# Key and query projections of the single-head layers as three products of rounded parts made on GpSimd

## The chip, the cores and the metric

The kernel runs on one core of one Trainium2 chip, as a single launch. The metric is the device time of that launch in microseconds (us); the figure for a kernel is the median of its runs. Engines are named PE (TensorE, matrix products; PEld is its weight loading), DVE (VectorE), ACT (ScalarE), POOL (GpSimd) and SP (SyncE, which only issues transfers here).

## The reference, cut to what matters

Four attention layers run one after another over 8 images of 128 channels and 1024 positions. The first two have 8 heads of 16 channels, the last two have one head of 128 channels. In a single-head layer, with `P = 128` channels `C` and `N = 1024` positions:

```python
h = _group_norm(x, gamma, beta).reshape(B, Cc, N)
q = jnp.einsum('oc,bcn->bon', wq, h) + bq[None, :, None]
k = jnp.einsum('oc,bcn->bon', wk, h) + bk[None, :, None]
v = jnp.einsum('oc,bcn->bon', wv, h) + bv[None, :, None]
attn = jax.nn.softmax(jnp.einsum('bcn,bcm->bnm', q, k) * scale, axis=-1)
out = jnp.einsum('bcm,bnm->bcn', v, attn)
return x + (jnp.einsum('oc,bcn->bon', wo, out) + bo[None, :, None]).reshape(B, Cc, H, W)
```

## The kernel before, in words

`many_heads` runs layers 0 and 1, `one_head` (line 847 on) layers 2 and 3. The change is in `one_head` alone. It goes through 16 images (2 layers of 8), in a software pipeline: while PE computes attention for one image, it also computes averages, keys, queries and values of the next one. The first image's keys and queries are made at the end of `many_heads`, so 15 images are projected in `one_head`.

The attention of one image is 8 tiles of 128 positions. In the order in which PE's queue is written out (`body` on line 1364), a tile m has: the scores of tile m+2 into `s_ps` (six products, since both operands are kept as a rounded part `HI` and a rest `LO` of type fp32r, and HI*HI, HI*LO and LO*HI are added), eight transposes of tile m's probabilities into `t_ps`, and a quarter of the output product `pv_ps` (six products again). DVE takes the maxima and the rests of the transposed probabilities (`rests`, line 1143). ACT computes exponentials, divides them by their sums and copies the rounded parts (line 1286).

Work for the next image shares one PSUM bank, `misc`, and is placed between these by a table on line 868: `"avg"` in tile 0, `"k0"` at the end of tile 1, `"k1"` at the end of tile 2, `"q0"` at the end of tile 3, `"v0"` in tile 5, `"q1"` at the end of tile 6, `"v1"` in tile 7. Here k0 is the first half (512 positions) of the keys, k1 the second. For the first image, two output products of layer 1 (`o0`, `o1`) are placed in tiles 3 and 4 as well.

How a projection comes about: PE averages the statistics (`average`), DVE computes the variance, POOL makes the scale and the shift (`coefficients`, line 1023), ACT normalises both halves of `x_in` into `h` (line 1229) and raises `h_ready`, PE waits for `h_ready` in front of k0 and computes `project` (line 1313), an fp32 product of 128x128 weights from `wg` with 128x512 of `h`. ACT adds the bias into `full` one tile later (`evacuate`, line 1242) and POOL splits the result into `HI` and `LO` (`split`, lines 1033 and 1034), which the scores of the next image read.

Every engine works through its own queue in order; semaphores join them.

Of the kernel before, what the change touches and what calls it, by code (L numbers as in the profile page):

```python
# [15 lines left out]
ALU = mybir.AluOpType  # L16
ACT = mybir.ActivationFunctionType
AX = mybir.AxisListType
F32 = mybir.dt.float32
BF16 = mybir.dt.bfloat16  # L20
F32R = mybir.dt.float32r

P = 128
T = 1024
B = 8
HALF = 512
# [820 lines left out]
def one_head(nc, ctx0, kept, w, bv, out):  # L847
# [24 lines left out]
    HI, LO = 0, 1  # L872
# [19 lines left out]
    with ctx:  # L892
        def sb(name, shape, dt=F32):
            return ctx.enter_context(nc.sbuf_tensor("o_" + name, shape, dt))
# [4 lines left out]
        def sem(name):  # L899
            return ctx0.enter_context(nc.semaphore("o_" + name))  # L900
# [8 lines left out]
        wg = [sb(f"wg{i}", [P, NW]) for i in range(2)]  # L909
        value_weights = kept["value_weights"]  # L910
        h = sb("h", [P, T])
        y = sb("y", [P, T])
        ident = sb("ident", [P, P])
        bst = sb("bst", [P, 2, 6])
# [43 lines left out]
        coef_ready = sem("coef_ready")  # L958
        scale_ready = sem("scale_ready")
        h_ready = sem("h_ready")  # L960
        x_dma = sem("x_dma")
        w_dma = [sem(f"w_dma{i}") for i in range(2)]
        o_dma = sem("o_dma")
# [54 lines left out]
        @block.gpsimd  # L1018
        def _(pool):
            own = Own(pool, pool_own)  # L1020
            nc.gpsimd.tensor_scalar(ident[:, :], kept["ident"][:, :], 1.0, None, ALU.mult).then_inc(consts, 1)

            def coefficients(n, par):

                pool.wait_ge(coef_ready, n)
                tt = nc.gpsimd.tensor_tensor
                own.done(tt(co[:, 4:5], co[:, 1:2], exponent[:, :], ALU.pow))
                own.done(tt(co[:, 2:3], co[:, 4:5], wg[par][:, W_GAMMA:W_GAMMA + 1], ALU.mult))
                own.done(tt(co[:, 5:6], gs[:, 0:1], co[:, 2:3], ALU.mult))
                tt(co[:, 3:4], wg[par][:, W_BETA:W_BETA + 1], co[:, 5:6], ALU.subtract).then_inc(scale_ready, 1)  # L1030

            def split(source, hi, lo, ready):
                own.done(nc.gpsimd.tensor_copy(hi, source))
                nc.gpsimd.tensor_tensor(lo, source, hi.bitcast(F32), ALU.subtract).then_inc(ready, 1)

            def split_kq(n, operand, name, c):
                pool.wait_ge(kq_full, n)
                cols = slice(c * HALF, (c + 1) * HALF)
                split(full[name][:, cols], operand[:, HI, cols], operand[:, LO, cols], kq_parts)

            def split_v(par, c):
                tiles = slice(c * HT, (c + 1) * HT)
                split(full["v"][:, c * HALF:(c + 1) * HALF].rearrange("p (s c) -> p s c", s=HT),
                      vT[par][:, HI, tiles, :], vT[par][:, LO, tiles, :], v_parts)

            def stage_g(u, par, finish=False):
                coefficients(u + 1, par)
                if finish:
                    pool.wait_ge(rrep_ready, 1)
                    own.done(nc.gpsimd.tensor_tensor(attn[:, :], kept["num"][:, :], kept["rrep"][:, :], ALU.mult))  # L1050
                    pool.sem_inc(attn_ready, 1)
                split_kq(4 * u + 1, k[par], "k", 0)
                split_kq(4 * u + 2, k[par], "k", 1)
                split_kq(4 * u + 3, q[par], "q", 0)
                pool.wait_ge(v_full, 2 * u + 1)
                split_v(par, 0)
                split_kq(4 * u + 4, q[par], "q", 1)
                pool.wait_ge(v_full, 2 * u + 2)
                split_v(par, 1)

            split_v(0, 0)
            split_v(0, 1)
            own.drain()

            def body(first=False, last=False):
                for u in range(2 - last):
                    stage_g(u, 1 - u, finish=first and u == 0)
                if not last:
                    pool.sem_inc(coef_ready, -2)
                    pool.sem_inc(kq_full, -8)  # L1070
                    pool.sem_inc(v_full, -4)
                own.drain()

            body(first=True)
            with pool.Fori(1, PAIRS - 1):
                body()
            body(last=True)

        @block.vector
# [229 lines left out]

        @block.tensor  # L1310
        def _(pe):
            def project(par, c, column):
                nc.tensor.matmul(misc[:, :], wg[par][:, column:column + P], h[:, c * HALF:(c + 1) * HALF],  # L1313
                                 start=True, stop=True).then_inc(misc_for_act, 1)

            def project_values(c):
                for n in range(4):
# [12 lines left out]
            def split_product(to, stationary, moving, start=True, stop=True):  # L1330

                pairs = ((HI, HI), (HI, LO), (LO, HI))
                for n, (a, b) in enumerate(pairs):
                    last = nc.tensor.matmul(to, stationary(a), moving(b), start=start and n == 0,  # L1334
                                            stop=stop and n == len(pairs) - 1)
                return last
# [26 lines left out]

            def body(first=False, last=False):
                places, _, before, taken = shared_bank(first, last)
                for m in range(BODY):
                    u, tile = m // TILES, m % TILES

                    def in_shared_bank(place):

                        name = places[u].get((tile, place))
                        if name is None:
                            return
                        reader, count = before[u, name]
                        pe.wait_ge(misc_act if reader == "act" else misc_dve, count)
                        if name == "avg":
                            pe.wait_ge(stats_ready, u + 1)
                            pe.wait_ge(w_dma[1 - u], 16)
                            combine_weights(nc, misc, wg[1 - u])
                            average()  # L1380
                        elif name == "o0":
                            pe.wait_ge(attn_ready, 1)
                            project_output(0)
                        elif name == "o1":
                            project_output(1)
                        elif name[0] == "v":
                            project_values(int(name[1]))
                        else:
                            if name == "k0":
                                pe.wait_ge(h_ready, u + 1)  # L1390
                            project(1 - u, int(name[1]), W_K if name[0] == "k" else W_Q)

                    pe.wait_ge(p_ready, m + 1)
                    if tile == 2:
                        pe.wait_ge(kq_parts, 4 * u + 1)
                    if tile == TILES - 2 and not (last and u == 1):
                        pe.wait_ge(kq_parts, 4 * u + 4)
                    if not (last and m >= BODY - 2):
                        scores((m + 2) // TILES % 2, m + 2)
                    in_shared_bank(0)  # L1400
                    for bank in range(2):
                        pe.wait_ge(t_free, 2 * m + bank + 1)
                        for n in range(HT):
                            st = bank * HT + n
                            transposed = nc.tensor.transpose(t_ps[bank][:, n, :], probs[m % 2][:, st * P:(st + 1) * P], ident[:, :])  # L1405
                        transposed.then_inc(t_ready, 1)
                    in_shared_bank(1)
                    if m >= HT or not first:
                        if m % HT == 0:
                            pe.wait_ge(pv_free, m // HT + 1)  # L1410
                        if tile == HT:
                            pe.wait_ge(v_parts, 2 * (u + 1))
                        products((m // HT + 3) % 4, m % HT)
                    in_shared_bank(2)
                pe.sem_inc(t_free, -2 * BODY)
                pe.sem_inc(pv_free, -4)
                pe.sem_inc(misc_dve, -taken["dve"])
                pe.sem_inc(misc_act, -taken["act"])
                if not last:
                    pe.sem_inc(p_ready, -BODY)  # L1420
                    pe.sem_inc(kq_parts, -8)
                    pe.sem_inc(v_parts, -4)
                    pe.sem_inc(stats_ready, -2)
                    pe.sem_inc(h_ready, -2)
                    pe.sem_inc(w_dma[0], -16)
                    pe.sem_inc(w_dma[1], -16)

# [102 lines left out]
```

## Time and profile before

| | |
|---|---|
| median of 3 runs | 2296.9 us (2295.36 to 2297.52) |
| span of the profiled execution | 2295.6 us; no other time of that execution is given |
| busy share of the span | PE 96%, PEld 42%, DVE 79%, ACT 75%, POOL 23% |
| `one_head` | about the last 580 us of the span |

The span runs from the first to the last instruction. A busy share is the time in which an engine had an instruction in it, over the whole span; the two halves of the kernel differ, so the rows below are read by stretch. The span lies 1.3 us below the median of the runs.

### The profile page before, as it was taken

What the parts mean: (1) busy time and instruction counts of PE and PEld (TensorE: products, weight loads), DVE (VectorE), ACT (ScalarE), POOL (GpSimd) and SP (SyncE); (2) the same over time, 40 slices, a digit from 0 to 9 for tenths busy, and PEclk for the clock granted to TensorE, in tenths of its full rate; (3) what the DMA queues carried; (4) which work ended last, traced back from release to release, by engine and by line L of the source; (5) the groups of instructions that cost most, each with busy time, mean ns of one, the idle gap of its engine ahead of it and who ended that gap; (6) DMA issues with size and microseconds to landing.
All of it is one profiled execution on the core that took longest, in us unless ns stands there. A gap on an engine that the chain in (4) does not pass through costs nothing. (4 is left out here: it accounts for less than half of the span.)

```text
span 2295.6 us, 34006 instructions
## 1 busy us (share of the span) xinstructions
PE 2201.2 (96%) x11776; PEld 972.2 (42%) x11776; DVE 1815.8 (79%) x3176; ACT 1719.9 (75%) x3107; POOL 520.6 (23%) x689
## 2 busy tenths in 40 slices
PE   3999999999999999999999999999989999999998
PEld 1223232323333232333333232333326888888887
DVE  2878888888888878888888888888837777777776
ACT  1467677777877777776767777776777888888887
POOL 3113030202213030311203020211113333333331
PEclk9999999999999999999999999999999999999999
DMA  6053351606244261616345160615112112121111
GB/s 82 7 70 53 58 78 35 104 22 91 41 69 66 45 90 36 95 27 84 50 61 76 36 103 22 94 37 75 26 31 72 53 48 66 36 65 57 42 53 49
DMA packets 81647, 132.31 MB, mean 58 GB/s; under 512 B 17632, under 2 KB 50528, under 8 KB 81504
## 3 DMA queue, kind: packets, MB, share of 16 engines
q1 hardware_dynamic: 78240, 129.70, 32.5%
q8 instruction: 79, 1.29, 0.3%
q10 hardware_dynamic: 3264, 0.79, 0.2%
q14 instruction: 64, 0.52, 0.1%
HBM read 53.12 MB, written 17.83 MB: 31 GB/s over the span
## 5 line engine op out<-in xcount | busy, mean ns | idle before, releaser
L447 DVE TENSOR_REDUCE h_half_nmax<-h_s_ps 128x1 f32<-128x512 f32 x2048 | 1285.8, 684 | 270.2 <-PE h_s_ps L682 263.0
L598 ACT ACTIVATE h_probs<-h_st_ps 128x512 f32<-128x512 f32 x2048 | 1103.7, 600 | 388.2 <-PE h_st_ps L819 382.2
L682 PE MATMUL h_s_ps<-h_krep,h_qrep 96*128 96x512 bf16 x2048 | 795.7, 389 | 22.4 <-SPq L232 20.8
L819 PE MATMUL h_st_ps<-h_qrep,h_krep 99*128 99x512 bf16 x2048 | 779.9, 382 | 35.1 <-DMA h_qrep<-h_mrow 24.3
L674 PE MATMUL h_pv<-h_probs,h_vT 128*32 128x512 f32 x4096 | 548.1, 607 | 0.9 <-ACT h_probs L598 0.7
L682 PEld LDWEIGHTS h_s_ps<-h_krep,h_qrep 96*128 96x128 bf16 x2048 | 200.0, 98 | 677.3 <-DVE h_half_nmax L447 503.0
L819 PEld LDWEIGHTS h_st_ps<-h_qrep,h_krep 99*128 99x128 bf16 x2048 | 201.7, 99 | 230.6 <-DMA h_qrep<-h_mrow 36.4
L347 POOL TENSOR_SCALAR h_nparts<-h_nmax 128x16 bf16<-128x16 f32 x64 | 16.4, 256 | 956.6 <-DVE h_nmax L455 956.6
L1334 PE MATMUL o_s<-o_k,o_q 128*128 128x512 f32 x768 | 225.7, 430 | 7.4 <-DVE o_q L1155 5.8
L1334 PE MATMUL o_pv<-o_pT,o_vT 128*128 128x512 f32 x768 | 208.1, 406 | 0.8 <-ACTq L1261 0.8
L1149 DVE TENSOR_TENSOR o_pT<-o_t,o_pT 128x512 fp32r<-128x512 f32 x256 | 164.5, 684 | 43.8 <-ACT o_pT L1286 41.4
L1135 DVE TENSOR_REDUCE o_nmax<-o_s 128x1 f32<-128x1024 f32 x128 | 156.4, 1222 | 51.1 <-PE o_s L1334 48.7
L1256 ACT ACTIVATE o_probs<-o_probs,o_rinv 128x1024 f32<-128x1024 f32 x128 | 147.7, 1154 | 38.0 <-DVE o_rinv L1141 22.6
L1334 PEld LDWEIGHTS o_s<-o_k,o_q 128*128 128x128 f32 x768 | 146.6, 191 | 66.5 <-issue 30.2
L674 PEld LDWEIGHTS h_pv<-h_probs,h_vT 128*32 128x32 f32 x4096 | 81.6, 108 | 219.0 <-ACT h_probs L598 158.8
L1250 ACT ACTIVATE o_probs<-o_s,o_bias 128x1024 f32<-128x1024 f32 x128 | 144.3, 1128 | 9.2 <-DVE o_bias L1136 8.7
L1334 PEld LDWEIGHTS o_pv<-o_pT,o_vT 128*128 128x128 f32 x768 | 135.0, 189 | 24.2 <-DVE o_pT L1149 1.2
L1286 ACT CAST o_pT<-o_t 128x512 fp32r<-128x512 f32 x256 | 135.0, 578 | 1.6 <-PE o_t L1405 1.6
L1405 PE MATMUL o_t<-o_ident,o_probs 128*128 128x128 f32 x1024 | 133.2, 273 | 2.3 <-DVE o_pT L1149 2.3
L1405 PEld LDWEIGHTS o_t<-o_ident,o_probs 128*128 128x128 f32 x1024 | 119.2, 141 | 21.0 <-issue 2.5
L648 PE MATMUL h_misc<-h_h,h_wg 128*128 128x512 f32 x136 | 73.7, 623 | 7.9 <-ACT h_h L542 5.4
L328 POOL TENSOR_TENSOR h_co<-h_co,exponent 128x1 f32<-128x1 f32 x17 | 9.7, 568 | 235.9 <-DVE h_co L413 235.9
(116 smaller groups left out, 1380.1 us busy)
## 6 DMA issues: line engine op xcount, KB each, us to landing
h_krep<-h_kp SPq DMA_DIRECT2D x96, 256.0 KB, 8.7
h_qrep<-h_qp SPq DMA_DIRECT2D x192, 128.0 KB, 9.5
x_res<-out_dram SPq DMA_DIRECT2D x24, 512.0 KB, 3.7
num<-av SPq DMA_DIRECT2D x128, 64.0 KB
rrep<-rden_dram SPq DMA_DIRECT2D x16, 512.0 KB
out_dram<-o_y SPq DMA_DIRECT2D x16, 512.0 KB
out_dram<-h_y SPq DMA_DIRECT2D x15, 512.0 KB, 2.6
o_x_in<-out_dram SPq DMA_DIRECT2D x15, 512.0 KB, 3.5
```

The lines of the kernel that those rows point to most:

```text
L447: reduce = nc.vector.tensor_reduce(half_nmax[:, c, unit:unit + 1], s_ps[bank(2 * n + c)][:, :], AX.X, ALU.max, negate=True)
L598: nc.scalar.activation(probs[g % 2][:, j, :], st_ps[bank(n)][:, :], ACT.Exp, scale=1.0 / CH ** 0.5).then_inc(exp_done, 1)
L674: product = nc.tensor.matmul(pv_ps[32 * j:32 * j + 32, :], vT[par][:, k % TILES, quad * QUAD + j, :], probs[k % 2][:, j, :], start=(k % TI ...
L682: nc.tensor.matmul(s_ps[bank(n)][:, :], qrep[par][0:KS, th, head, tile * P:(tile + 1) * P], krep[par][0:KS, head, c * HALF:(c + 1) * HALF] ...
L819: nc.tensor.matmul(st_ps[bank(n)][:, :], krep[par][0:KM, head, st * P:(st + 1) * P], qrep[par][0:KM, th, head, :], start=True, stop=True). ...
L1135: own.done(nc.vector.tensor_reduce(nmax[:, b:b + 1], s_ps[b][:, :, :], AX.XY, ALU.max, negate=True))
L1149: nc.vector.tensor_tensor(pt[:, LO, :, :][to], t_ps[bank][:, :, :], pt[:, HI, :, :][to].bitcast(F32), ALU.subtract).then_inc(t_free, 1)
L1250: nc.scalar.activation(probs[b][:, :], s_ps[b][:, :, :], ACT.Exp, bias=bias[:, b:b + 1], scale=SCALE, accum_out=rsum[:, b:b + 1]).then_inc ...
L1256: nc.scalar.activation(probs[b][:, :], probs[b][:, :], ACT.Copy, scale=rinv[:, b:b + 1]).then_inc(p_ready, 1)
L1286: nc.scalar.copy(pT[m // HT % 2][:, HI, bank * HT:(bank + 1) * HT, m % HT * P:(m % HT + 1) * P], t_ps[bank][:, :, :]).then_inc(hi_ready, 1)
L1334: last = nc.tensor.matmul(to, stationary(a), moving(b), start=start and n == 0, stop=stop and n == len(pairs) - 1)
L1405: transposed = nc.tensor.transpose(t_ps[bank][:, n, :], probs[m % 2][:, st * P:(st + 1) * P], ident[:, :])
```

## The change

Keys and queries are no longer one fp32 product. The weights of keys and queries (128x256) and the normalised `h` (128x1024) are each split into `HI` and `LO` parts of type fp32r, and `project` adds three products of them. POOL makes the parts in the new function `split_projection`: the weights' parts right after the coefficients, then, after a wait for `h_ready`, those of `h` in two halves, each of which raises `h_parts_ready`. PE waits for the first half in front of k0 and for the second in front of k1. The values are still projected from `h` in fp32.

```diff
@@ -909,6 +909,8 @@
         wg = [sb(f"wg{i}", [P, NW]) for i in range(2)]
         value_weights = kept["value_weights"]
         h = sb("h", [P, T])
+        h_parts = sb("h_parts", [P, 2, T], F32R)
+        w_parts = sb("w_parts", [P, 2, 2 * P], F32R)
         y = sb("y", [P, T])
         ident = sb("ident", [P, P])
         bst = sb("bst", [P, 2, 6])
@@ -958,6 +960,7 @@
         coef_ready = sem("coef_ready")
         scale_ready = sem("scale_ready")
         h_ready = sem("h_ready")
+        h_parts_ready = sem("h_parts_ready")
         x_dma = sem("x_dma")
         w_dma = [sem(f"w_dma{i}") for i in range(2)]
         o_dma = sem("o_dma")
@@ -1043,8 +1046,19 @@
                 split(full["v"][:, c * HALF:(c + 1) * HALF].rearrange("p (s c) -> p s c", s=HT),
                       vT[par][:, HI, tiles, :], vT[par][:, LO, tiles, :], v_parts)
 
+            def split_projection(u, par):
+
+                weights = wg[par][:, 0:2 * P]
+                own.done(nc.gpsimd.tensor_copy(w_parts[:, HI, :], weights))
+                own.done(nc.gpsimd.tensor_tensor(w_parts[:, LO, :], weights, w_parts[:, HI, :].bitcast(F32), ALU.subtract))
+                pool.wait_ge(h_ready, u + 1)
+                for c in range(2):
+                    cols = slice(c * HALF, (c + 1) * HALF)
+                    split(h[:, cols], h_parts[:, HI, cols], h_parts[:, LO, cols], h_parts_ready)
+
             def stage_g(u, par, finish=False):
                 coefficients(u + 1, par)
+                split_projection(u, par)
                 if finish:
                     pool.wait_ge(rrep_ready, 1)
                     own.done(nc.gpsimd.tensor_tensor(attn[:, :], kept["num"][:, :], kept["rrep"][:, :], ALU.mult))
@@ -1067,6 +1081,7 @@
                     stage_g(u, 1 - u, finish=first and u == 0)
                 if not last:
                     pool.sem_inc(coef_ready, -2)
+                    pool.sem_inc(h_ready, -2)
                     pool.sem_inc(kq_full, -8)
                     pool.sem_inc(v_full, -4)
                 own.drain()
@@ -1309,9 +1324,10 @@
 
         @block.tensor
         def _(pe):
-            def project(par, c, column):
-                nc.tensor.matmul(misc[:, :], wg[par][:, column:column + P], h[:, c * HALF:(c + 1) * HALF],
-                                 start=True, stop=True).then_inc(misc_for_act, 1)
+            def project(c, column):
+                cols = slice(c * HALF, (c + 1) * HALF)
+                split_product(misc[:, :], lambda part: w_parts[:, part, column:column + P],
+                              lambda part: h_parts[:, part, cols]).then_inc(misc_for_act, 1)
 
             def project_values(c):
                 for n in range(4):
@@ -1386,9 +1402,9 @@
                         elif name[0] == "v":
                             project_values(int(name[1]))
                         else:
-                            if name == "k0":
-                                pe.wait_ge(h_ready, u + 1)
-                            project(1 - u, int(name[1]), W_K if name[0] == "k" else W_Q)
+                            if name in ("k0", "k1"):
+                                pe.wait_ge(h_parts_ready, 2 * u + int(name[1]) + 1)
+                            project(int(name[1]), W_K if name[0] == "k" else W_Q)
 
                     pe.wait_ge(p_ready, m + 1)
                     if tile == 2:
@@ -1421,7 +1437,7 @@
                     pe.sem_inc(kq_parts, -8)
                     pe.sem_inc(v_parts, -4)
                     pe.sem_inc(stats_ready, -2)
-                    pe.sem_inc(h_ready, -2)
+                    pe.sem_inc(h_parts_ready, -4)
                     pe.sem_inc(w_dma[0], -16)
                     pe.sem_inc(w_dma[1], -16)
```

## Rows read from the trace of the kernel before

**Rows 1.** Busy time in a stretch, one image long (engine, instructions; granted clock)

```profile
1873.37:1908.44 35.07, 35.07 (x192) 28.62 (x191) 27.21 (x54) 30.99 (x49) 12.55 (x17) 1.00 0.17 55
```

**Rows 2.** Groups by line, PE, 1760 to 2250 us (busy, mean ns | idle before)

```profile
L1313 PE MATMUL o_misc<-o_h,o_wg 128*128 128x512 f32 x112 | 57.2, 592 | 0.0
```

**Rows 3.** Timeline of PE, a tile without projection (start, length, instruction)

```profile
1890.57 1.04 PE L1405 MATMUL o_t<-o_ident,o_probs 128*128 128x128 f32 x8
1891.37 1.63 PE L1334 MATMUL o_pv<-o_pT,o_vT 128*128 128x512 f32 x6
1892.83 1.55 PE L1334 MATMUL o_s<-o_k,o_q 128*128 128x512 f32 x6
1894.22 1.04 PE L1405 MATMUL o_t<-o_ident,o_probs 128*128 128x128 f32 x8
```

**Rows 4.** Timeline of all engines, from the coefficients to the first keys' parts

```profile
1911.31 0.19 POOL L1030 TENSOR_TENSOR o_co<-o_wg,o_co 128x1 f32<-128x1 f32 x1
1911.54 1.53 ACT L1229 ACTIVATE o_h<-o_x_in,o_co 128x512 f32<-128x512 f32 x2 [0.87 <-POOL o_co L1030]
...
1912.11 1.04 PE L1405 MATMUL o_t<-o_ident,o_probs 128*128 128x128 f32 x8
...
1914.37 1.02 PE L1313 MATMUL o_misc<-o_h,o_wg 128*128 128x512 f32 x2
...
1914.92 1.29 DVE L1149 TENSOR_TENSOR o_pT<-o_t,o_pT 128x512 fp32r<-128x512 f32 x2 [1.19 <-ACT o_pT L1286]
...
1916.37 0.70 ACT L1242 ACTIVATE full_k<-o_misc,o_wg 128x512 f32<-128x512 f32 x1
...
1916.61 1.03 PE L1405 MATMUL o_t<-o_ident,o_probs 128*128 128x128 f32 x8
...
1917.25 0.61 POOL L1033 CAST o_k<-full_k 128x512 fp32r<-128x512 f32 x1 [5.75 <-ACTq L1245]
...
1917.94 1.30 POOL L1034 TENSOR_TENSOR o_k<-full_k,o_k 128x512 fp32r<-128x512 f32 x1
```

**Rows 5.** The same timeline, one image later

```profile
1946.59 1.52 ACT L1229 ACTIVATE o_h<-o_x_in,o_co 128x512 f32<-128x512 f32 x2 [0.75 <-POOL o_co L1030]
...
1949.37 0.59 PE L1313 MATMUL o_misc<-o_h,o_wg 128*128 128x512 f32 x1
```

**Rows 6.** Timeline of PE, the first two products after a wait

```profile
1728.47 0.72 PE L1334 MATMUL o_s<-o_k,o_q 128*128 128x512 f32 x2 [1.65 <-ACT o_probs L1256]
...
1728.79 0.40 PE L1334 MATMUL o_s<-o_k,o_q 128*128 128x512 f32 x1
```

**Rows 7.** Timeline of all engines, first image of the single-head layers

```profile
1735.49 1.52 ACT L1229 ACTIVATE o_h<-o_x_in,o_co 128x512 f32<-128x512 f32 x2 [0.76 <-POOL o_co L1030]
...
1737.17 0.30 PEld L1313 LDWEIGHTS o_misc<-o_h,o_wg 128*128 128x128 f32 x2 [0.93 <-issue]
...
1740.31 0.70 ACT L1242 ACTIVATE full_k<-o_misc,o_wg 128x512 f32<-128x512 f32 x1
1740.39 2.37 POOL L1050 TENSOR_TENSOR attn<-num,rrep 128x1024 f32<-128x1024 f32 x1 [4.94 <-SPq L989]
...
1745.11 0.70 PE L1324 MATMUL o_misc<-attn,wo 128*128 128x512 f32 x1 [0.68 <-ACTq L1244]
```

**Rows 8.** Timeline of all engines, where the single-head layers begin

```profile
1717.89 2.30 POOL L1034 TENSOR_TENSOR o_vT<-full_v,o_vT 128x512 fp32r<-128x512 f32 x1
1718.98 2.29 DVE L1155 TENSOR_TENSOR o_q<-full_q,o_q 128x1024 fp32r<-128x1024 f32 x1
```

**Rows 9.** Timeline of PE in the multi-head layers, waits

```profile
857.28 0.39 PE L819 MATMUL h_st_ps<-h_qrep,h_krep 99*128 99x512 bf16 x1 [1.91 <-DMA h_qrep<-h_mrow]
...
1061.16 0.39 PE L819 MATMUL h_st_ps<-h_qrep,h_krep 99*128 99x512 bf16 x1 [1.81 <-DMA h_qrep<-h_mrow]
```

**Rows 10.** Busy time in stretches of the multi-head layers, granted clock third from last

```profile
160.00:1060.00 900.00, 882.34 (x4824) 280.38 (x4821) 757.25 (x1283) 673.32 (x1290) 179.04 (x239) 1.00 0.41 62
...
1061.00:1066.00 5.00, 4.83 (x18) 1.25 (x19) 2.02 (x4) 2.22 (x4) 0.00 (x0) 0.66 0.37 139
```

## The prediction

> **What bounds the kernel now.** The change is in the single-head layers, so I read those by stretch, not the whole span. First the busy times of a stretch that is one image long: PE is busy for all of its 35.07 us, at full clock (1.00), while DVE has 27, ACT 31 and POOL 12.6 us of work [rows 1]. Then the groups by line on PE: over 490 us the projections had no idle time in front of them, so no wait ends late there [rows 2]. So in a settled image PE's own work is the time: what leaves PE's queue shortens the image, and a wait in PE's queue lengthens it by as much, since there is no slack to absorb it. The third view is the timeline, for two questions: what one projection costs on PE, and how soon after `h` is ready PE reads it.
>
> **The change part by part.**
>
> *The products.* Between the transposes of two tiles without a projection PE takes 1894.22 - 1890.57 = 3.65 us [rows 3]; with k0 in between, 1916.61 - 1912.11 = 4.50 us [rows 4]. An fp32 projection thus costs 0.85 us. It becomes three fp32r products of 128x512, a form that the kernel already uses, each with a weight load of its own: six for the scores take 1894.22 - 1892.83 = 1.39 us, six for the output 1892.83 - 1891.37 = 1.46 us [rows 3], so 0.232 to 0.243 each, and three 0.70 to 0.73. I take the scores (same operands, same two-part pattern): a saving of 0.155 us a projection, with bounds of 0.12 (the output's pace) and 0.17 (the reading of four times to a hundredth). Four projections an image: 0.62 us (0.48 to 0.68).
>
> *The weights' parts.* POOL begins them when the coefficients are done, 1911.31 + 0.19 = 1911.50 [rows 4]. Subtractions of 128x512 take 1.30 us [rows 4] and a two-input operation of 128x1024 2.37 [rows 7], so 256 columns come to about 0.75 us; the cast is under the 0.61 us of 512 columns. With 0.08 us between instructions (0.69 from cast to subtraction, less 0.61 [rows 4]) they end by 1913.1 at the latest. ACT normalises until 1911.54 + 1.53 = 1913.07 and POOL hears of it some 0.1 us later (below). So I cost them at nothing: the normalisation covers them. Were it shorter, all that sticks out would add to the wait that follows.
>
> *The wait.* k0 now follows not ACT but ACT and then POOL. From the end of the normalisation: the signal to POOL; 0.69 us to the start of the subtraction; 1.30 us of subtraction; the signal to PE; and the slower first product after a pause, whose successor follows after 0.32 us [rows 6] where 0.23 is the pace, so 0.09. For the signals the rows give 0.04 us (POOL to ACT, 1911.50 to 1911.54 [rows 4]), 0.16 (ACT to PE, 1737.01 to 1737.17 [rows 7]) and 0.18 (ACT to POOL, 1917.07 to 1917.25 [rows 4]). I take 0.16 for ACT to POOL, where two semaphore steps lie in between as for PE, and 0.09 for POOL to the product, as the instruction itself raises that semaphore. Sum: 0.16 + 0.69 + 1.30 + 0.09 + 0.09 = 2.33 us. So k0 could start at 1913.07 + 2.33 = 1915.40 and started at 1914.37 [rows 4]: 1.03 us late. In the next image it is 1946.59 + 1.52 + 2.33 = 1950.44 against 1949.37 [rows 5]: 1.07. Mean 1.05 us. Lower bound with both signals at 0.04 and no slow restart, 0.78; upper with 0.18 and 0.19, 1.17.
>
> Behind the wait in PE's queue stand k0, the scores of tile 4 and all that follows, so the image gets longer by it. ACT's evacuation of k0 was at 1916.37, after its exponentials [rows 4]; three products from 1915.40 end about 1916.3, so ACT hardly waits. POOL's parts of the second half of `h` follow the first at once and end 1915.22 + 0.03 + 0.69 + 1.30 = 1917.24; k1 comes a tile later, 4.5 us after k0, and finds them. POOL stood idle for 5.75 us until 1917.25 [rows 4]; the new work fills just that, and the keys' own parts come 0.9 us later, still in time. No transfer is added or moved.
>
> *A settled image:* 1.05 - 0.62 = +0.43 us. There are 14 of them: 14.7 us of waits (10.9 to 16.4) less 8.7 us of products (6.7 to 9.5), +6.0 us.
>
> *The first image* differs. There PE already waits for `h`: its weights load at 1737.17, right behind the normalisation [rows 7], and k0 comes 2.1 us later than that. But o0 waits for ACT (0.68 us idle) [rows 7], and ACT, which reached k0's bias at 1740.31 [rows 7], would get it about 0.6 us later: the half-rate products from 1739.3 on end near 1740.9. So most of the lateness dissolves in front of o0. On POOL the product of `num` and `rrep` (2.37 us, until 1742.76 [rows 7]) now stands behind the parts: 1741.2 + 2.4 = 1743.6, still 1.5 us ahead of o0 at 1745.11. With its products saved I take +0.5 us, between 0 and 3.
>
> *Sum:* 2295.6 + 6.0 + 0.5 = 2302.1 us for the profiled execution, and with the 1.3 us by which the median lies above it, 2303.4 us. The bounds together: +1.4 to +12.7, so 2298.3 to 2309.6.
>
> **A rule against the change.** Where POOL subtracted beside a DVE operation with two SBUF inputs, 128x512 took 2.30 us [rows 8] instead of 1.30; beside DVE's `rests`, which read one operand from PSUM, later images show 1.30 [rows 4]. The Trainium skill, GPSIMD Engine Reference, section Key points, says that GpSimd shares its SBUF interfaces with VectorE and is contended by DVE instructions in a two-port mode or with two SBUF inputs; the trace agrees. By the rule alone the parts of `h` would suffer only if such an instruction fell beside them; it is a rival below.
>
> **The rivals.**
>
> *The parts are in time, faster.* The mechanism is a shorter chain between normalisation and k0. It breaks even where k0 is 0.6 us late and gives more than 0.2% where it is under 0.26 late, that is with 1.5 us in place of 2.33. With no wait at all the time would be 2296.9 - 8.7 - 0.6 = 2287.6 us. For it: POOL idles before the keys' parts, and its spans are rough. Against: cast and subtraction are serial, 2.0 us between them, while only 1914.37 - 1913.07 = 1.30 us lie between the normalisation's end and k0 [rows 4].
>
> *POOL and DVE in each other's way.* 1.0 us more in the first subtraction, 14 times: 2317 us. Against: DVE has maxima and `rests` from PSUM in that stretch [rows 4].
>
> *The products don't get shorter*, because three weight loads hold them: the waits stay, 2296.9 + 14.7 + 0.5 = 2312 us. Against: the scores load weights for every product too [rows 3].
>
> *The clock.* After a PE wait of 1.81 us at 1061.16 [rows 9] the next 5 us had a mean clock of 0.66 [rows 10], so about 3.4 us at 1.2 GHz, which costs some 1.7 us. Were that to follow every k0: 14 x 1.7 = 24 us, 2327. Against: twelve PE waits of over 1 us lie between 160 and 1060 us, the longest 1.91 us at 857.28 [rows 9], and there the clock was 1.00 throughout [rows 10].
>
> **How the numbers follow.** A measurement of this kernel can tell about 0.2%, 4.6 us, from no change. Forecast 0.78; in time 0.07; contention 0.05; products no shorter 0.05; clock 0.05. The predicted time is the forecast's, 2303.4. Its bounds, 2298.3 to 2309.6, cross the line of "slower" at 2301.5: some 0.20 of its 0.78 lies below. Slower: 0.58 + 0.15 = 0.73; same: 0.20 and 0.01 of the first rival; faster: 0.06. The range goes from 2298, the forecast's lower end, to 2313, which takes in unshortened products; contention, clock and a clear gain stay outside, 0.17 in all.
>
> **What would show it.** A wait of about 1 us in front of k0 in every image, with POOL's L1034 as its releaser, and nearly none elsewhere on PE; settled images of about 35.5 us in place of 35.07; three products a projection at 0.23 us; POOL's subtraction of `h` at 1.30 us; the clock at 1.00. The prediction is wrong if PE shows no wait at k0, if the subtraction takes 2 us or more, or if ACT becomes what PE waits for.

## The result and the profile after

The changed kernel takes 2303.97 us (median of 10 runs, 2298.7 to 2306.95) against 2297.21 us of the kernel before, measured beside it (10 runs, 2294.01 to 2299.34). The ratio is 1.0029 with a 95% interval of 1.0020 to 1.0038: slower by 6.8 us, where 6.5 was forecast. The profiled execution spans 2302.3 us; 2302.1 was worked out.

Busy time and clock of two settled images after the change (the view of [rows 1]: length, PE, PEld, DVE, ACT, POOL, granted clock):

```profile
1877.00:1912.37 35.37, 34.43 (x195) 29.19 (x195) 26.91 (x55) 31.04 (x49) 17.35 (x22) 1.00 0.16 53
1912.37:1947.82 35.45, 34.62 (x197) 29.37 (x197) 26.84 (x53) 31.16 (x49) 17.34 (x22) 1.00 0.17 54
```

PE has idle time now, 0.8 to 0.9 us in each image, and nothing fills it: an image takes longer although PE has less to do. POOL has 17.35 us of work in place of 12.55. The clock stays at 1.00. The waits on PE, 1765 to 2255 us (who waited for whom: total, times, longest):

```profile
PE o_misc L1350 <- POOL o_h_parts L1037: 11.9, 14, 0.9
```

This is PE's only listed wait in that stretch: once in each of 14 images, and the releaser is POOL's subtraction. The timeline of all engines around k0, to be held against [rows 4]:

```profile
1914.51 0.40 POOL L1052 CAST o_w_parts<-o_wg 128x256 fp32r<-128x256 f32 x1
1914.61 1.52 ACT L1244 ACTIVATE o_h<-o_x_in,o_co 128x512 f32<-128x512 f32 x2 [0.87 <-POOL o_co L1033]
...
1914.99 0.73 POOL L1053 TENSOR_TENSOR o_w_parts<-o_wg,o_w_parts 128x256 fp32r<-128x256 f32 x1
1915.19 1.04 PE L1421 MATMUL o_t<-o_ident,o_probs 128*128 128x128 f32 x8
...
1916.31 0.61 POOL L1036 CAST o_h_parts<-o_h 128x512 fp32r<-128x512 f32 x1 [0.59 <-ACTq L1251]
...
1917.00 1.28 POOL L1037 TENSOR_TENSOR o_h_parts<-o_h,o_h_parts 128x512 fp32r<-128x512 f32 x1
...
1918.42 0.94 PE L1350 MATMUL o_misc<-o_h_parts,o_w_parts 128*128 128x512 f32 x3 [0.83 <-POOL o_h_parts L1037]
...
1919.20 1.56 PE L1350 MATMUL o_s<-o_k,o_q 128*128 128x512 f32 x6
...
1919.43 0.70 ACT L1257 ACTIVATE full_k<-o_misc,o_wg 128x512 f32<-128x512 f32 x1
...
1920.60 1.04 PE L1421 MATMUL o_t<-o_ident,o_probs 128*128 128x128 f32 x8
```

The chain reads off directly: ACT ends at 1914.61 + 1.52 = 1916.13, POOL casts from 1916.31 and subtracts until 1918.28, and PE starts at 1918.42. The weights' parts were done at 1915.72, and POOL then idled for 0.59 us: the normalisation covers them. From transposes to transposes the tile with k0 takes 5.41 us, 0.91 more than before. A tile with k1, whose parts are ready when PE comes to it, in PE's timeline:

```profile
1920.60 1.04 PE L1421 MATMUL o_t<-o_ident,o_probs 128*128 128x128 f32 x8
...
1922.85 0.85 PE L1350 MATMUL o_misc<-o_h_parts,o_w_parts 128*128 128x512 f32 x3
1923.54 1.56 PE L1350 MATMUL o_s<-o_k,o_q 128*128 128x512 f32 x6
1924.94 1.04 PE L1421 MATMUL o_t<-o_ident,o_probs 128*128 128x128 f32 x8
```

It takes 4.34 us where a tile with an fp32 projection took 4.50 [rows 4]: three products in 0.69 us, and 0.16 us saved.

### The profile page after: what moved, and what is told of

The parts are those of the page before. It is cut to its first block and busy times, and to the rows that moved or that the text cites. A ratio compares the mean times of both kernels' runs of the same rounds, so it can differ in the third digit from the quotient of the medians.

```text
span 2302.3 us, 34253 instructions
## 1 busy us (share of the span) xinstructions
PE 2194.1 (95%) x11836; PEld 983.7 (43%) x11836; DVE 1812.4 (79%) x3176; ACT 1721.8 (75%) x3107; POOL 592.5 (26%) x779
## 3 DMA queue, kind: packets, MB, share of 16 engines
q8 instruction: 79, 1.29, 0.3%
## 5 line engine op out<-in xcount | busy, mean ns | idle before, releaser
L1350 PE MATMUL o_s<-o_k,o_q 128*128 128x512 f32 x768 | 201.9, 399 | 7.4 <-DVE o_q L1170 5.7
```

## The experiments

Besides the ratio, which goes against the kernel before measured beside it, each is read by the length of its settled images in one profiled execution. From the 2nd to the 15th average on PE (the product with `gmat`) there are 13 of them:

| kernel | 2nd average | 15th average | one image, us | ratio, interval |
|---|---|---|---|---|
| before | 1768.99 | 2224.42 | 35.03 | 1 |
| changed | 1770.64 | 2230.81 | 35.40 | 1.0029 (1.0020 to 1.0038) |
| k0 later | 1774.79 | 2228.72 | 34.92 | 0.9996 (0.9987 to 1.0005) |
| wait alone | 1772.06 | 2240.87 | 36.06 | 1.0073 (1.0059 to 1.0087) |
| parts alone | 1767.28 | 2222.71 | 35.03 | 1.0003 (0.9994 to 1.0012) |
| weights late | 1773.96 | 2262.28 | 37.56 | 1.0158 (1.0145 to 1.0172) |
| parts sooner | 1770.05 | 2221.45 | 34.72 | 0.9976 (0.9964 to 0.9988) |
| sooner and order | 1766.30 | 2213.40 | 34.39 | 0.9954 (0.9937 to 0.9971) |
| order alone | 1771.53 | 2226.47 | 35.00 | 1.0002 (0.9990 to 1.0013) |
| two inputs beside | 1769.25 | 2233.46 | 35.71 | 1.0043 (1.0029 to 1.0057) |

The theory: PE's time in a settled image is its own work, less what three products save, plus how late POOL's parts come. The rivals: the products save nothing, or POOL's work costs by disturbing others.

### The wait alone

```diff
-                split_product(misc[:, :], lambda part: w_parts[:, part, column:column + P],
-                              lambda part: h_parts[:, part, cols]).then_inc(misc_for_act, 1)
+                nc.tensor.matmul(misc[:, :], wg[par][:, column:column + P], h[:, c * HALF:(c + 1) * HALF],
+                                 start=True, stop=True).then_inc(misc_for_act, 1)
```

> GpSimd makes the parts and PE waits for them in front of k0 and k1, but the projection is the old fp32 product. If wait and saving are separate and add up, every settled image is about 1.07 us longer than before: 14 x 1.07 + some 2 us of the first image = +17 us, ratio 1.0074. If the split products save nothing, it is like the changed kernel, 1.003.

Measured 1.0073. In PE's timeline k0 is the old pair of fp32 passes behind the new wait:

```profile
1808.13 0.28 PE L1343 MATMUL o_misc<-o_st,gmat 128*128 128x2 f32 x2
...
1814.34 1.10 PE L1328 MATMUL o_misc<-o_h,o_wg 128*128 128x512 f32 x2 [0.80 <-POOL o_h_parts L1037]
...
1844.24 0.28 PE L1343 MATMUL o_misc<-o_st,gmat 128*128 128x2 f32 x2
```

A settled image is 36.06 - 35.03 = 1.03 us longer: that is the wait. The changed kernel's is 36.06 - 35.40 = 0.66 us shorter than this one: that is what the products save, 0.165 us each. That 1.03 and -0.66 add up to the change's +0.37 is no test by itself, since both are differences to this one kernel. But the tiles with k1, q0 and q1, where PE waits in neither kernel, agree with the second term: they take 4.34 us in the changed kernel and 4.50 to 4.51 here, in the mean of the settled images. So "the products save nothing" falls.

### The parts alone

PE and POOL get a semaphore each from ACT, so PE waits as before and nobody waits for the parts; PE reads the fp32 input.

```diff
+                act.sem_inc(h_for_pe, 1)
...
-                            if name in ("k0", "k1"):
-                                pe.wait_ge(h_parts_ready, 2 * u + int(name[1]) + 1)
+                            if name == "k0":
+                                pe.wait_ge(h_for_pe, u + 1)
```

> GpSimd makes the parts, nobody waits for them and nobody reads them; the projection is the old fp32 product behind the old wait. If GpSimd's work costs nothing by itself, ratio 1.000 within 0.001 and no idle time on PE. If it disturbs VectorE at the shared interfaces, VectorE's operations beside it get longer and the ratio rises towards 1.003.

Measured 1.0003, settled images as before to a hundredth, and no wait on PE in 465 us. DVE's `rests` kept their length, 684 ns in the mean in the kernel before and 685 here (groups by line, 1770 to 2235 us, before and this run):

```profile
L1149 DVE TENSOR_TENSOR o_pT<-o_t,o_pT 128x512 fp32r<-128x512 f32 x214 | 137.5, 684 | 37.8 <-ACT o_pT L1286 35.7
L1165 DVE TENSOR_TENSOR o_pT<-o_t,o_pT 128x512 fp32r<-128x512 f32 x212 | 136.3, 685 | 41.2 <-ACT o_pT L1303 39.3
```

One settled image of this run (the view of [rows 1]):

```profile
1802.27:1837.35 35.08, 35.08 (x192) 28.63 (x191) 27.12 (x54) 30.91 (x49) 17.36 (x22) 1.00 0.18 54
```

POOL works 4.8 us more than in [rows 1], and PE is busy all the time: the parts cost nothing by themselves.

### The weights' parts behind the wait

```diff
                 weights = wg[par][:, 0:2 * P]
+                pool.wait_ge(h_ready, u + 1)
                 own.done(nc.gpsimd.tensor_copy(w_parts[:, HI, :], weights))
                 own.done(nc.gpsimd.tensor_tensor(w_parts[:, LO, :], weights, w_parts[:, HI, :].bitcast(F32), ALU.subtract))
-                pool.wait_ge(h_ready, u + 1)
```

> The changed kernel with the weights' parts made behind the wait for the normalised input, not ahead of it. If the normalisation covered them, all of it now sticks out: 0.40 + 0.73 us and two gaps of 0.07, 1.26 us an image, 15 x 1.26 = 19 us on top of the change, ratio to the kernel before 1.011. If PE's wait had other causes than GpSimd's chain, 1.003 as before.

The direction held: PE's wait in front of k0 rose from 0.8 or 0.9 to between 2.0 and 2.1 us. But 1.0158 is half as much again as 1.011. Five of the 13 settled images take 36.56 to 36.68 us, as expected (35.40 + 1.26 = 36.66); the other eight take 38.13 to 38.20, some 1.6 us more. PE's timeline in one image of 36.58 us, in one of 38.13 us and in one of 36.64 us, and the busy times of two stretches behind k0 (granted clock third from last):

```profile
1781.38 0.94 PE L1350 MATMUL o_misc<-o_h_parts,o_w_parts 128*128 128x512 f32 x3 [2.02 <-POOL o_h_parts L1037]
1782.15 1.56 PE L1350 MATMUL o_s<-o_k,o_q 128*128 128x512 f32 x6
...
1930.94 1.34 PE L1350 MATMUL o_misc<-o_h_parts,o_w_parts 128*128 128x512 f32 x3 [2.02 <-POOL o_h_parts L1037]
1932.08 2.75 PE L1350 MATMUL o_s<-o_k,o_q 128*128 128x512 f32 x6
...
1969.15 0.93 PE L1350 MATMUL o_misc<-o_h_parts,o_w_parts 128*128 128x512 f32 x3 [2.09 <-POOL o_h_parts L1037]
```

```profile
1930.90:1937.00 6.10, 6.06 (x24) 4.91 (x25) 2.27 (x5) 3.54 (x5) 3.61 (x4) 0.72 0.00 0
1969.10:1975.00 5.90, 5.85 (x30) 4.94 (x31) 3.47 (x7) 4.45 (x7) 3.65 (x4) 1.00 0.00 0
```

Behind the wait of 2.02 us at 1930.94 the clock was 0.72 in the mean, so part of that stretch ran at 1.2 GHz: six scores took 2.75 us, not 1.56. Behind the wait of 2.09 us at 1969.15 it stayed at 1.00, and behind another of 2.02 us at 1781.38 the scores took their 1.56 us. So the prediction's clock rival is real, and its price was nearly right: 1.6 us where 1.7 stood. Here it came behind eight of 13 waits of 2.0 to 2.1 us, and the length of the wait does not tell which. Behind the 0.8 to 0.9 us that the change brings it did not come in a settled image.

### k0 in the next place of the table

k0 goes behind the scores of tile 2, and ACT reads it in the same tile as before.

```diff
-    PLACES = {"avg": (0, 1), "k0": (1, 2), "k1": (2, 2), "q0": (3, 2), "v0": (5, 1),
+    PLACES = {"avg": (0, 1), "k0": (2, 0), "k1": (2, 2), "q0": (3, 2), "v0": (5, 1),
```

> k0 is placed behind the scores of tile 2 (1.39 us later on PE); all else as in the changed kernel. If the wait at k0 is the only loss and a split projection saves about 0.165 us, the wait goes and all 60 projections save: 15 x 4 x 0.165 = 9.9 us, ratio to the kernel before 0.9957, settled images of about 34.4 us. If the split products save nothing, 1.000. If the loss comes from GpSimd's extra work disturbing other engines, it stays above 1.

A miss: 0.9996, settled images of 34.92 us, not 34.4. By the ratio alone this would be "the split products save nothing", but the tile with k1 takes 4.34 us here too. The wait at k0 is gone, but another stands in its place (timeline of PE, then of ACT, in the image where it is largest):

```profile
1952.86 1.62 PE L1351 MATMUL o_pv<-o_pT,o_vT 128*128 128x512 f32 x6
1954.76 1.65 PE L1351 MATMUL o_s<-o_k,o_q 128*128 128x512 f32 x6 [0.29 <-ACT o_probs L1272]
1956.26 0.86 PE L1351 MATMUL o_misc<-o_h_parts,o_w_parts 128*128 128x512 f32 x3
```

```profile
1953.56 1.15 ACT L1272 ACTIVATE o_probs<-o_probs,o_rinv 128x1024 f32<-128x1024 f32 x1 [0.20 <-ACT o_h L1245]
```

Six output products take 1.46 us, so the scores that follow could start at 1954.32; they wait until 1954.76 for ACT's division, which ends at 1954.71 because ACT has just normalised. Where k0 stood between the two, it filled that time: in the kernel before, the division ended at 1913.27 + 1.15 = 1914.42, just behind k0's start at 1914.37 [rows 4]. Moving k0 away uncovers the gap.

This is not all. The waits of PE's weight loading show the same releaser 27 times from 1770 to 2235 us, twice an image:

```profile
PEld o_s L1351 <- ACT o_probs L1272: 12.0, 27, 0.7
```

One is the place shown; its tile takes 4.52 to 4.91 us, 4.67 in the mean, where the tile with k1 takes 4.34. The other is the tile without a projection, with 3.88 us where the changed kernel takes 3.62. Together these are 0.59 us, and 34.92 less 0.59 is 34.33 us, which is what most images take in the run below that has both sooner parts and the new order. In the second place (timeline of PE, then of ACT) the scores could start at 1967.88, and ACT's division ends at 1967.96:

```profile
1966.42 1.62 PE L1351 MATMUL o_pv<-o_pT,o_vT 128*128 128x512 f32 x6
1968.01 1.65 PE L1351 MATMUL o_s<-o_k,o_q 128*128 128x512 f32 x6
```

```profile
1966.81 1.15 ACT L1272 ACTIVATE o_probs<-o_probs,o_rinv 128x1024 f32<-128x1024 f32 x1 [0.20 <-ACT full_q L1258]
```

Why ACT is late there is not shown; in this image it had to wait 0.38 us for k0's products two tiles before.

### The parts sooner

The keys' weights alone are split ahead of the input, the queries' after it, and ACT signals each half of `h` with the instruction itself.

```diff
-                own.mark(nc.scalar.activation(h[:, cols], x_in[:, cols], ACT.Identity, bias=co[:, 3:4],
-                                              scale=co[:, 2:3]))
+                nc.scalar.activation(h[:, cols], x_in[:, cols], ACT.Identity, bias=co[:, 3:4],
+                                     scale=co[:, 2:3]).then_inc(h_ready, 1)
...
+                split_weights(W_K)
                 for c in range(2):
+                    pool.wait_ge(h_ready, 2 * u + c + 1)
                     cols = slice(c * HALF, (c + 1) * HALF)
                     split(h[:, cols], h_parts[:, HI, cols], h_parts[:, LO, cols], h_parts_ready)
+                split_weights(W_Q)
+                pool.sem_inc(h_parts_ready, 1)
```

> k0 stays at the end of tile 1, but GpSimd's chain starts sooner: only the keys' weights are split ahead of the input, the queries' weights after it, and ScalarE signals each normalised half by itself. The first half is done 0.7 us sooner, so k0's lateness falls from 1.07 to some 0.35 us and nothing is put between the old places: settled images 35.40 - 0.7 = 34.7 us, ratio to the kernel before about 0.998. If PE is held by ScalarE at the scores behind k0, as with k0 in tile 2, about 35.0 us and 1.000.

Measured 0.9976 and 34.72 us an image, as expected; the rival with ACT falls, since POOL is the only releaser of PE's waits in 465 us:

```profile
PE o_misc L1354 <- POOL o_h_parts L1037: 2.1, 11, 0.4
```

### The order of the products alone, and with the parts sooner

The changed kernel's `split_product` takes HI*HI, HI*LO, LO*HI of weights and input; here the input's rest comes last and has a wait of its own.

```diff
+                if rounded is not None:
+                    pe.wait_ge(h_rounded, rounded)
+                product(HI, HI, start=True, stop=False)
+                product(LO, HI, start=False, stop=False)
+                if whole is not None:
+                    pe.wait_ge(h_parts_ready, whole)
+                product(HI, LO, start=False, stop=True).then_inc(misc_for_act, 1)
```

> The changed kernel with the order of the products alone: two products of 0.23 us run under GpSimd's subtraction, so the wait of k0 falls by about 0.5 us: settled images 35.40 - 0.54 = 34.9 us, ratio to the kernel before 1.000 (between 0.999 and 1.001). If PE's lateness at k0 is taken up elsewhere, no change from the changed kernel, 1.003.

> As the run with sooner parts, and the three products are ordered so that the rest of the input comes last: k0's first two products need only its rounded part, and PE waits for the rest in front of the third. The wait at k0 should go altogether: settled images of about 34.4 us, 15 x 0.66 = 9.9 us saved less some 1 to 2 us in the first image, ratio 0.9963. If ScalarE has become the bound, as the run with k0 in tile 2 suggests, no better than 34.8 us and 0.999.

The order alone gives 1.0002 and 35.00 us, as expected; PE waits 0.5 us at most in front of the third product (waits on PE, 1770 to 2235 us):

```profile
PE o_misc L1333 <- POOL o_h_parts L1060: 5.8, 14, 0.5
```

Both together give 0.9954 and 34.39 us, which beats the kernel before by 0.46% (interval 0.29 to 0.63%) and the changed one too. The timeline of all engines around k0:

```profile
1907.16 0.61 POOL L1061 CAST o_h_parts<-o_h 128x512 fp32r<-128x512 f32 x1 [0.22 <-ACT o_h L1252]
...
1907.85 1.15 ACT L1278 ACTIVATE o_probs<-o_probs,o_rinv 128x1024 f32<-128x1024 f32 x1
...
1907.95 1.30 POOL L1063 TENSOR_TENSOR o_h_parts<-o_h,o_h_parts 128x512 fp32r<-128x512 f32 x1 [0.18 <-POOL o_h_parts L1061]
...
1909.03 0.85 PE L1337 MATMUL o_misc<-o_h_parts,o_w_parts 128*128 128x512 f32 x3
```

k0 starts at 1909.03, before the subtraction ends at 1909.25: its first product runs under it. From 1770 to 2235 us no wait is listed on PE, as before the change. What is left is small: the tile with k0 takes 4.33 to 4.54 us, 4.39 in the mean, against 4.34 with k1. The scores behind k0 find ACT's division done, here at 1909.00.

### The changed kernel once more

> The changed kernel once more, beside the others on the same chip: ratio to the kernel before 1.003.

1.0028 (1.0016 to 1.0040), settled images of 35.40 us.

### A VectorE operation with two SBUF inputs beside the parts

The result of the added operation is read by nobody.

```diff
+                    if tile == 1 and not first_it and not last_it:
+                        own.done(nc.vector.tensor_tensor(unused[:, :], kept["num"][:, 0:HALF], kept["rrep"][:, 0:HALF], ALU.add))
```

> The changed kernel with one more VectorE addition of 128x512 from two SBUF tensors in tile 1, whose result nobody reads, put behind the maximum so that it falls beside GpSimd's cast and subtraction of the first half. If the two engines' SBUF interfaces exclude each other, as at the handover where the subtraction took 2.30 us, GpSimd's two instructions together take 0.5 to 1.0 us more and k0 comes that much later: 14 x 0.5 to 1.0 = 7 to 14 us over the changed kernel, ratio to the kernel before 1.006 to 1.009. If they don't meet, 1.003 as before, since VectorE has idle time there.

Measured 1.0043, less than expected. The interval, 1.0029 to 1.0057, takes in the 1.003 of "they don't meet", so the ratio does not decide; the settled images do, which are 0.31 us longer than the changed kernel's. The timeline of all engines:

```profile
1916.25 0.61 POOL L1037 CAST o_h_parts<-o_h 128x512 fp32r<-128x512 f32 x1 [0.58 <-ACTq L1254]
...
1916.66 0.75 DVE L1205 TENSOR_TENSOR o_unused<-num,rrep 128x512 f32<-128x512 f32 x1
1916.94 1.60 POOL L1038 TENSOR_TENSOR o_h_parts<-o_h,o_h_parts 128x512 fp32r<-128x512 f32 x1
...
1918.68 0.94 PE L1353 MATMUL o_misc<-o_h_parts,o_w_parts 128*128 128x512 f32 x3 [1.15 <-POOL o_h_parts L1038]
```

POOL's subtraction takes 1.60 us, 0.31 more, where DVE's addition lies beside its first 0.47 us. The cast, beside which DVE's addition begins, keeps its 0.61. The images grew by just those 0.31 us. So the two engines do get in each other's way, at a lower price than expected. Only part of the addition fell beside the subtraction, which may be why; that is not shown. DVE's own operations in that stretch don't bring it about: in the changed kernel POOL's subtractions of `h` take 1.286 us in the mean (groups by line, 1765 to 2255 us):

```profile
L1037 POOL TENSOR_TENSOR o_h_parts<-o_h,o_h_parts 128x512 fp32r<-128x512 f32 x28 | 36.0, 1286 | 2.2
```

## Why the prediction was right

*PE's own work is the time of a settled image.* Right: with no wait the image with all four projections split is 34.39 us, 0.64 shorter; with the wait alone 1.03 longer.

*The products save 0.155 us each, 0.62 an image.* Measured 0.66 between the wait alone and the changed kernel, so 14 x 0.66 = 9.2 us for 8.7.

*k0 is 1.05 us late.* Measured 1.03 by the wait alone, 14.4 us for 14.7. By its parts, in the timeline shown: 0.18 us to POOL (0.16), 0.69 (0.69), 1.28 (1.30), 0.14 to PE (0.09), and 1919.20 - 1918.42 = 0.78 us for three products that take 0.69 elsewhere, so 0.09 for the restart (0.09). Sum 2.38, where 2.33 stood.

*The weights' parts cost nothing.* Right, with 0.59 us to spare; behind the wait they stick out.

*A settled image: +0.43.* Measured +0.37, 14 x 0.37 = 5.1 us for 6.0.

*The first image: +0.5, between 0 and 3.* In range, but the step behind the number did not hold. From its average to the next it took 1768.99 - 1732.38 = 36.61 us before and 1770.64 - 1732.18 = 38.46 after: +1.85. Counted from the average, k0 came 2.10 us later, as forecast, and ACT reached it 0.65 us later (0.6). But the lateness did not dissolve in front of o0: o0 came at 1747.13 - 1732.18 = 14.95 us, not 1745.11 - 1732.38 = 12.73, so 2.22 us later. Before the change PE had only 0.68 us of idle time between k0 and o0 that could take it up, and after the change ACT waited for PE there (timeline of PE and ACT):

```profile
1739.10 1.62 PE L1350 MATMUL o_misc<-o_h_parts,o_w_parts 128*128 128x512 f32 x3 [2.82 <-POOL o_h_parts L1037]
...
1740.52 2.76 PE L1350 MATMUL o_s<-o_k,o_q 128*128 128x512 f32 x6
...
1744.17 1.18 ACT L1301 CAST o_pT<-o_t 128x512 fp32r<-128x512 f32 x2 [1.38 <-PE o_t L1421]
...
1747.13 1.13 PE L1340 MATMUL o_misc<-attn,wo 128*128 128x512 f32 x2 [0.31 <-ACTq L1259]
```

The clock had a part in it. Busy times from 1738 to 1744 us, of the kernel before and of the changed one (granted clock third from last):

```profile
1738.00:1744.00 6.00, 6.00 (x23) 4.28 (x22) 3.97 (x7) 5.80 (x10) 3.37 (x3) 0.76 0.37 105
```

```profile
1738.00:1744.00 6.00, 4.90 (x14) 3.96 (x15) 2.13 (x4) 4.07 (x7) 5.75 (x5) 0.50 0.37 106
```

PE waited for 2.82 us in front of this stretch and into it, and the clock was at half in all of it. In the second profile of the changed kernel the same image took 37.20 us, +0.59, so this term moves from one execution to the next by more than its forecast size. In the first profile the 0.9 us too much for the settled images and the 1.35 too little here nearly cancel, and that the total agrees so closely is partly luck.

*The rivals.* Parts in time: not in the changed kernel, but in the version with parts sooner and order, and it gave a ratio of 0.9954 (0.9937 to 0.9971) where 2287.6 of 2296.9 us, 0.996, was worked out. Contention: not in the changed kernel (POOL's subtractions of `h` took 1.286 us in the mean), and worth 0.3 rather than 1.0 us when forced. Products no shorter: excluded by the 0.66 us and by the tiles with k1. (The weight loads that the prediction holds against it stand in [rows 1], 191 for 192 products, and not in [rows 3].) Clock: not behind waits of 0.8 to 0.9 us in settled images, in eight of 13 images behind 2.0 to 2.1.

The Trainium skill, GPSIMD Engine Reference, section Key points, had named DVE instructions with two SBUF inputs as what contends with GpSimd. The forced case agrees (1.60 us against 1.29), and so does the absence of it beside `rests`, which read one operand from PSUM.

## What to carry to other kernels

Where one engine's own work is the time, cheaper operands pay only if the engine that makes them delivers as early as the old operand came; add up the new chain from the last common event to the first reader, signals and restart included, before counting what is saved. A late operand was better met here by shortening that chain (smaller first pieces, a signal for each half, the late part used last) than by moving its reader, because the reader was itself filling another engine's latency. Here the same saving of 0.165 us a projection was a loss of 0.3% with the first order of work and a gain of 0.46% with the second.

## What the runs showed of the hardware

Waits of 2.0 to 2.1 us on PE, once in each image, were followed by stretches at half clock (1.2 GHz) in eight of 13 images and by full clock in five, at 1.6 us for each fall; waits of the same 2.02 us stood before both. Waits of 0.8 to 0.9 us were never followed by half clock in the settled images. A POOL subtraction of two SBUF tensors that met 0.47 us of a DVE operation with two SBUF inputs took 0.31 us longer, while a POOL cast with one input, which met 0.20 us of it, did not.
